# Cross-attention of 16 batches: a scale of v for each group, beta added in two parts, and g made ahead of the third and fourth products

## The reference

```python
q = jnp.einsum('bte,ef->btf', emb, Wq) + bq
k = jnp.einsum('bml,le->bme', latent, Wk) + bk
v = jnp.einsum('bml,le->bme', latent, Wv) + bv
w = jnp.einsum('bte,bme->btm', q, k) * scale
w = jax.nn.softmax(w, axis=1)
pred = jnp.einsum('btm,bme->bte', w, v)
x = pred + emb
mu = jnp.mean(x, axis=-1, keepdims=True)
var = jnp.var(x, axis=-1, keepdims=True)
return (x - mu) * jax.lax.rsqrt(var + EPS) * gamma + beta
```

## Time and profile before

| | |
|---|---|
| median of 3 runs | 228.85 us (227.89 to 231.82) |
| the profiled execution | 228.07 us, its span 226.2 us |
| mean granted clock of TensorE, of full speed | 0.957 |
| busy in the span: PE, DVE, ACT, POOL | 190.5 us (84%), 169.3 (75%), 162.7 (72%), 142.0 (63%) |
| moved from and to HBM | 22.15 MB read, 16.78 MB written |

### The profile page before, as it was taken

How to read it: one execution, slowest core, us unless ns; L and a number is a source line. 1 busy time by engine, 2 the same in 40 slices (tenths; PEclk the granted TensorE clock), 3 DMA queues, 4 the chain that set the end, 5 groups by cost and what they waited for, 6 DMA issues and landing times.

```text
span 226.2 us, 3278 instructions
## 1 busy us (share of the span) xinstructions
PE 190.5 (84%) x1003; PEld 117.6 (52%) x1003; DVE 169.3 (75%) x403; ACT 162.7 (72%) x336; POOL 142.0 (63%) x149
## 2 busy tenths in 40 slices
PE   6994998899996999999999999999999969696100
PEld 6993655465554565656565656555656535342000
DVE  0698138979899896959695969586958686879891
ACT  2745638378968797978797879787978876748730
POOL 1010005103994969696969696969696969698991
PEclk9999599999999999999999999999999999999855
DMA  5999940014018090909090909090909090404175
GB/s 220 315 313 250 398 198 1 3 14 172 0 81 293 0 346 28 352 22 351 23 355 17 352 19 351 23 336 36 348 26 352 19 351 25 185 0 187 67 294 197
DMA packets 9277, 39.14 MB, mean 173 GB/s; under 512 B 812, under 2 KB 2732, under 8 KB 5420
## 3 DMA queue, kind: packets, MB, share of 16 engines
...
HBM read 22.15 MB, written 16.78 MB: 172 GB/s over the span
## 4 chain that ended last, share of the span: by engine, by line
PE 40%; POOL 16%; DVE 14%; ACT 9%; issue 8%; DMA 7%; SPq 2%; POOLq 1%; ACTq 0%; DVEq 0%
PE s_ps L400 16%; DMA ctx_nat<-in_ctx 7%; POOL obuf L925 7%; PE xT_ps L371 6%; POOL obuf L931 5%; PE a_ps L363 5%; PE a_ps L390 4%; PE b_ps L390 4%; DVE obuf L721 4%; PE cg_ps L352 4%; ACT xT L501 3%; ACT obuf L534 2%; POOL rstd L954 2%; ACT prob_part L513 2%; DVE obuf L746 2%
## 5 line engine op out<-in xcount | busy, mean ns | idle before, releaser
L925 POOL TENSOR_TENSOR obuf<-obuf,gamma_all 128x512 f32<-128x512 f32 x43 | 54.2, 1276 | 24.9 <-ACT obuf L534 24.9
L400 PE MATMUL s_ps<-xT,gT 128*120 128x512 f32 x128 | 58.9, 604 | 0.0
L931 POOL TENSOR_TENSOR obuf<-obuf,beta_all 128x1536 f32<-128x1536 f32 (+1 forms) x15 | 49.6, 3306 | 1.2
L501 ACT ACTIVATE xT<-xT_ps 128x512 f32<-128x512 f32 x64 | 34.6, 593 | 17.3 <-PE xT_ps L371 17.3
L534 ACT ACTIVATE obuf<-obuf,shift,rstd 128x512 f32<-128x512 f32 x43 | 33.4, 813 | 9.0 <-POOL shift L958 9.0
L371 PEld LDWEIGHTS xT_ps<-ident,xbuf 128*128 128x128 f32 x256 | 30.1, 142 | 15.1 <-issue 8.0
L371 PE MATMUL xT_ps<-ident,xbuf 128*128 128x128 f32 x256 | 34.0, 275 | 3.8 <-ACT xT L501 3.8
L400 PEld LDWEIGHTS s_ps<-xT,gT 128*120 128x120 f32 x128 | 23.5, 188 | 25.6 <-issue 23.7
L528 ACT ACTIVATE square_junk<-obuf,y_sum 128x512 f32<-128x512 f32 x46 | 32.8, 716 | 0.0
L390 PE MATMUL b_ps<-v_part,prob_part 120*128 120x512 f16 x90 | 24.5, 381 | 4.9 <-DVE obuf L721 4.9
L680 DVE TENSOR_REDUCE s_max<-s_ps 120x1 f32<-120x512 f32 x16 | 11.0, 689 | 20.3 <-PE s_ps L400 20.3
...
## 6 DMA issues: line engine op xcount, KB each, us to landing
...
```

Of the source, the lines that this page charges most:

```text
L400: mm = pe.matmul(s_ps[0:M, :], gT[:, b // 2 % 2, e, b % 2 * M:(b % 2 + 1) * M], xT[:, e, :], start=(e == 0), stop=(e == EC - 1))
L501: act.activation(xT[:, e, :].rearrange("p (j q) -> p j q", q=P), xT_ps[e % 2][:], ACT.Copy)\
L925: pool.tensor_tensor(obuf[:, b % ORING, j, :], obuf[:, b % ORING, j, :], gamma_all[:], ALU.mult)\
L931: pool.tensor_tensor(obuf[:, b % ORING, 0:n, :], obuf[:, b % ORING, 0:n, :], beta_all[:].unsqueeze(1).broadcast_to([P, n, E]), ALU.add)\
```

## The change

**The scales of v.** v gets a scale for each group of contexts: `onto_v`, `back_y` and `bv_scaled` have four columns or rows. So group 0's are made from the bounds of context 0, Wv and bv alone, and those of groups 1 to 3 in a second pass, behind v of batch 0. The loads of wv, bv and x of batch 1 go ahead of contexts 2 and 3. The bound of context 1 moves from ACT to DVE, those of contexts 2 and 3 move on ACT into round 1. ACT makes the high part of wv ahead of round 1's copies of x. POOL reduces three times, and its key products wait for the second pass. DVE's three further rows `bv_scaled` are made at the end of round 2.

**The round.** On PE, g comes ahead of the third and fourth products, v follows them directly (in round 15, v of batch 15 ahead of that of batch 14, for which `nth_v` counts), and the turning of the context moves into the scores, between the second and the third of their four steps. On ACT and DVE the parts of v come ahead of those of the context. On DVE the second residual comes ahead of the centring. On POOL beta is added to two tiles ahead of the statistics and to the third behind them; the store waits for both.

```diff
             load_x(0)
+            sp.dma_start(wv[:], Wv.rearrange("(c p) e -> p c e", p=P)).then_inc(wv_in, 16)
+            sp.dma_start(bv_all[:], bv.partition_broadcast(P)).then_inc(bv_in, 16)
             load_ctx(1)
-            sp.dma_start(wv[:], Wv.rearrange("(c p) e -> p c e", p=P)).then_inc(wv_in, 16)
+            load_x(1)
             load_ctx(2)
             load_ctx(3)
-            sp.dma_start(bv_all[:], bv.partition_broadcast(P)).then_inc(bv_in, 16)
-            load_x(1)
             load_x(2)
             sp.dma_start(gamma_all[:], gamma.partition_broadcast(P)).then_inc(gamma_in, 16)
             sp.dma_start(beta_all[:], beta.partition_broadcast(P)).then_inc(beta_in, 16)
...
-                sp.wait_ge(pool_out, b + 1)
+                sp.wait_ge(pool_out, 2 * (b + 1))
                 sp.wait_ge(dve_out, dve_units_before(b + 1))
                 sp.dma_start(out[b].rearrange("(p j) e -> p j e", j=RJ), obuf[:, b % ORING])\
                     .then_inc(stored[b % ORING], 16)
...
-            def scores(b):
+            def scores(b, next_pair=None):
+
                 if b > 0:
                     pe.wait_ge(prob_low, b)
                 for e in range(EC):
+                    if e == 2 and next_pair is not None:
+                        pe.wait_ge(ctx_in_sem[2 * next_pair // IN_GROUP], 16)
+                        turn_ctx(next_pair)
                     pe.wait_ge(g_copied, EC * (b // 2) + e + 1)
                     pe.wait_ge(xT_copied, EC * b + e + 1)
...
-                if last >= 0:
-                    product(last, 2)
-                    product(last, 3)
                 if s == 1:
                     context_g(1, 0, cg_ps)
                     context_g(1, 1, b_ps)
                 elif s < B - 2:
                     context_g(s // 2 + 1, s % 2, cg_ps)
-                context_v(s - 1)
+                if last >= 0:
+                    product(last, 2)
+                    product(last, 3)
                 if s == B - 1:
                     context_v(s)
-                if s % 2 == 1 and (s + 3) // 2 < PAIRS:
-                    pe.wait_ge(ctx_in_sem[(s + 3) // IN_GROUP], 16)
-                    turn_ctx((s + 3) // 2)
-                scores(s)
+                context_v(s - 1)
+                scores(s, (s + 3) // 2 if s % 2 == 1 and (s + 3) // 2 < PAIRS else None)
```

ACT and DVE, in the start and in the rounds:

```diff
-            bound_ctx(1)
             qk_to_high(3)
             ctx_to_high(1)
             copy_xT(0, 0)
-            bound_ctx(2)
             copy_xT(0, 1)
             act.wait_ge(back_g_done, 1)
-            act.wait_ge(dots_done, LC + 1 + EC)
+            act.wait_ge(dots_done, 1 + LC + 1)
             copy_g(0, 0, a_ps)
             copy_xT(0, 2)
             copy_xT(0, 3)
+            act.wait_ge(dots_done, LC + EC)
             copy_g(0, 1, b_ps)
-            bound_ctx(3)
+            act.wait_ge(wv_in, 16)
+            act.wait_ge(scales_done, 2)
+            act.activation(wv_part[:, HIGH], wv[:], ACT.Copy, scale=scale[:, S_WV:S_WV + 1]).then_inc(wv_high, 1)
...
                 if s == 1:
-                    act.wait_ge(scales_done, 2)
-                    act.activation(wv_part[:, HIGH], wv[:], ACT.Copy, scale=scale[:, S_WV:S_WV + 1]).then_inc(wv_high, 1)
+                    bound_ctx(2)
                 probs_to_high(s - 1)
                 copy_xT(s, 2)
                 copy_xT(s, 3)
+                if s == 1:
+                    bound_ctx(3)
                 if norm >= 0:
                     normalise(norm, 1)
                     normalise(norm, 2)
@@ -593,11 +603,13 @@
                     copy_g(s // 2 + 1, s % 2, cg_ps)
                 if y >= 0:
                     square(y, 0)
+                if s == B - 1:
+                    v_to_high(s)
+                v_to_high(s - 1)
+                if s == 1:
+                    act.wait_ge(scales_done, 3)
                 if s % 2 == 1 and (s + 3) // 2 < PAIRS:
                     ctx_to_high((s + 3) // 2)
-                v_to_high(s - 1)
-                if s == B - 1:
-                    v_to_high(s)
...
             key_dot(0)
-            softmax_bias(0)
+            dve.wait_ge(ctx_in_sem[1], 16)
+            dve.tensor_reduce(own_bound[0:M, B_CTX1:B_CTX1 + 1], ctx_nat[:, IN_GROUP:2 * IN_GROUP, 0:L], AX.XY, ALU.add,
+                              apply_absolute_value=True).then_inc(own_ctx, 1)
             dve.wait_ge(max_bounds, 2)
             dve.wait_ge(bv_bounded, 1)
...
+            dve.tensor_copy(bound[:, S_WV:S_WV + 1], max_bound[:, B_WV:B_WV + 1])
+            scales(dve.scalar_tensor_tensor(bound[:, S_V0:S_V0 + 1], max_bound[:, B_CTX0:B_CTX0 + 1],
                                             max_bound[:, B_WV:B_WV + 1], bv_bound[:], ALU.mult, ALU.add))
-            exact_scales(S_CTX1, S_V + 1)
+            exact_scales(S_WV, S_V0 + 1)
             dve.wait_ge(scales_done, 2)
-            softmax_scale(0)
+            scales(dve.tensor_tensor(back_v[:, 0:1], back[:, S_CTX0:S_CTX0 + 1], back[:, S_WV:S_WV + 1], ALU.mult))
+            dve.tensor_scalar(onto_v[:, 0:1], back_v[:, 0:1], scale[:, S_V0:S_V0 + 1], None, ALU.mult)\
+                .then_inc(back_v_done, 1)
+            dve.tensor_scalar(back_y[:, 0:1], back[:, S_V0:S_V0 + 1], 1.0 / PROB_SCALE, None, ALU.mult)\
+                .then_inc(back_v_done, 1)
+            dve.tensor_scalar(bv_scaled[:, 0], bv_all[:], scale[:, S_V0:S_V0 + 1], None, ALU.mult)\
+                .then_inc(back_v_done, 1)
+            softmax_bias(0)
             dve.wait_ge(wv_high, 1)
...
+            dve.wait_ge(max_bounds, 3)
+            dve.tensor_copy(bound[:, S_CTX1:S_CTX1 + 3], max_bound[:, B_CTX1:B_CTX1 + 3])
+            scales(dve.tensor_scalar(bound[:, S_V1:S_V1 + 3], max_bound[:, B_CTX1:B_CTX1 + 3],
+                                     max_bound[:, B_WV:B_WV + 1], bv_bound[:], ALU.mult, ALU.add))
+            exact_scales(S_CTX1, S_V1 + 3)
+            dve.wait_ge(scales_done, 3)
+            dve.tensor_scalar(back_g[:, 1:GROUPS], back[:, S_CTX1:S_CTX1 + 3], back[:, S_QK:S_QK + 1], None,
...
                 softmax_bias(s - 1)
                 residual(y, 0)
                 softmax_scale(s - 1)
+                residual(y, 1)
                 if norm >= 0:
                     center(norm, RJ - 1, norm + 1)
-                residual(y, 1)
                 probs_to_low(s - 1)
                 residual(y, 2)
                 residual(y, 3)
                 if norm >= 0:
...
+                if s == IN_GROUP + 1:
+                    dve.wait_ge(back_v_done, 2 + 3 + GROUPS - 1)
+                if s == B - 1:
+                    copy_v(s)
                 copy_v(s - 1)
                 statistics(y)
+                if s == B - 1:
+                    v_to_low(s)
+                v_to_low(s - 1)
                 if s % 2 == 1 and (s + 3) // 2 < PAIRS:
                     ctx_to_low((s + 3) // 2)
-                v_to_low(s - 1)
-                if s == B - 1:
-                    copy_v(s)
-                    v_to_low(s)
...
+                if s == 2:
+                    for g in range(1, GROUPS):
+                        dve.tensor_scalar(bv_scaled[:, g], bv_all[:], scale[:, S_V1 + g - 1:S_V1 + g], None, ALU.mult)\
+                            .then_inc(back_v_done, 1)
```

POOL:

```diff
-            pool.wait_ge(own_late, 1)
+            pool.wait_ge(own_wv, 1)
+            pool.partition_all_reduce(max_bound[:, B_WV:B_CTX1], own_bound[:, B_WV:B_CTX1], P,
+                                      bass.bass_isa.ReduceOp.max).then_inc(max_bounds, 1)
             pool.wait_ge(own_ctx, GROUPS - 1)
             pool.partition_all_reduce(max_bound[:, B_CTX1:], own_bound[:, B_CTX1:], P,
...
+            pool.wait_ge(back_v_done, 5)
             key_multiply(1)
             key_multiply(2)
...
-            def plus_beta(b):
-                n = pool_units(b)
-                pool.wait_ge(pool_gamma, units_before(b + 1))
-                pool.tensor_tensor(obuf[:, b % ORING, 0:n, :], obuf[:, b % ORING, 0:n, :],
-                                   beta_all[:].unsqueeze(1).broadcast_to([P, n, E]), ALU.add)\
+            def plus_beta(b, first, end):
+                pool.wait_ge(pool_gamma, units_before(b) + end)
+                pool.tensor_tensor(obuf[:, b % ORING, first:end, :], obuf[:, b % ORING, first:end, :],
+                                   beta_all[:].unsqueeze(1).broadcast_to([P, end - first, E]), ALU.add)\
                     .then_inc(pool_out if b < B - 2 else last_out[b - B + 2][0], 1)
 
             def finish_statistics(b):
@@ -963,11 +998,13 @@
                     key_multiply(s)
                 if s >= 3:
                     times_gamma(s - 3)
-                    plus_beta(s - 3)
+                    plus_beta(s - 3, 0, 2)
                 finish_statistics(s - 2)
+                if s >= 3:
+                    plus_beta(s - 3, 2, 3)
             finish_statistics(B - 1)
             times_gamma(B - 2)
-            plus_beta(B - 2)
+            plus_beta(B - 2, 0, 1)
```

(1 more changed line is left out.)

77 lines of the change are left out of this document (39 added, 38 removed).

## The result

| | before | after |
|---|---|---|
| median of 4 runs, us | 228.84 (227.89 to 231.82) | 216.63 (216.36 to 216.84) |
| profiled execution: span, us | 226.2 | 214.8 |
| round 1 starts at | 31.13 | 24.83 |
| round 5 starts at | 77.85 | 69.70 |
| round 13 starts at | 167.86 | 159.79 |

The ratio is 0.948 [0.945, 0.951] (the brackets are a 95% interval): faster, and faster than the range that was given. The direction and the wait were foretold, the sizes not: 222.5 was forecast. Executions more than 1.5% above the fastest of their kernel count in the medians of this document, not in its ratios.

A forecast was written before the change was run, and what follows sets the result against it. PE's round and POOL's loop, about equally long, were taken to bound the kernel. After the change, with x's ring setting pairs, 182.9 + 5 L gave 219.9, 6.3 under the 226.2 span; 228.85 - 6.3 = 222.5 us, range 218 to 227.5.

The forecast's parts named there:

- the wait: Odd rounds from 7: PE idle about 1 us at the first transposes, released by the DMA of x.
- the first rival: Middle rounds: x is not late, PE sets the pair at 21.98; 217.9 on the runs' scale; chance 0.2.
- The start: Before round 1: PE's 3.55 us stand goes and the clock is 2.4 GHz, saving 1.2 and 1.35; sum 6.1.
- The fourth product's wait: PE's round: the fourth product's 0.49 wait for DVE's second residual goes; a v wait of 0.46 comes.
- POOL's loop: POOL's round: splitting beta cuts it from 11.1 to about 10.2 us, so it no longer binds.
- the ring of x: Middle rounds: squares, statistics, beta's third tile, store, then load of x; 15.62 + L sets the pair, at 23.0.
- PE's loss to x: Odd rounds: x ready at 23.0 while PE is at 21.98, so PE waits about 1.0 us.
- L: Landing time of a load of x on SP's queue: 7.4 us, the median of 16 loads.
- the sum: Whole span: 71.85 + 4 x (15.62 + L) + (14.15 + L) + 34.4 = 182.9 + 5 L; 219.9 at L = 7.4.
- Net 0.1 given back: Up to round 5: new DVE work and an ACT wait, 1.5 + 1.2 + 0.6, against 3.2 saved; bounds 0 and 3.
- the 34.4: From round 15's start to the span's end: 36.17 less 2.52 plus 0.75.
- 0.23 a round: PE's new order: a pair of 21.98 against 22.44, a gain if PE sets it.

The follow-up runs named there:

- lf_both_old: Changed kernel with x's load ahead of the store, g back behind the third and fourth products and centring back ahead of the second residual: 216.84 us, ratio 0.949.
- load_first: Changed kernel with each load of x put ahead of the store before it on SP's queue: 214.60 us, ratio 0.937 to the kernel before.
- beta_one_load_first: Changed kernel with beta added in one part ahead of the statistics and x's load ahead of the store: 221.15 us, ratio 0.964.
- start_only: Changed kernel with every move inside the rounds and beta's split taken back, leaving the scale of v per group: 221.86 us, ratio 0.967.
- beta_one: Changed kernel with beta added in one part again, ahead of POOL's statistics: 220.83 us, ratio 0.964 to the kernel before.
- beta_one_dot_early: Changed kernel with beta in one part and the key dot of batch 3 moved from the end of round 3 to round 2's: 220.24 us, ratio 0.959.
- lf_turn_first: Changed kernel with x's load ahead of the store and the context's turning back ahead of the scores, round 1 apart: 214.93 us, ratio 0.940.
- lf_g_late: Changed kernel with x's load ahead of the store and g back behind the third and fourth products: 212.75 us, ratio 0.930.
- lf_centre_first: Changed kernel with x's load ahead of the store and the centring back ahead of the second residual: 214.76 us, ratio 0.939.

## Why the prediction was wrong

It was 5.9 us too high: 5.1 in the span, and 0.8 because it put the median above the profiled execution, as before; the profiled execution of after took 216.64, its median. Of the 5.1, 2.15 are before round 5, 2.4 in rounds 5 to 14 and 0.5 at the end. The result is also below the 217 to 219 of the first rival, in which x is not late: it lies in the 0.06 that was left for a kernel faster than all.

**Right: the mechanism.** The start lost its wait and its half clock (6.3 us, forecast as 6.1). The fourth product's wait became v's (0.32 by its row in lf_both_old, 0.30 in load_first, each with some 0.17 of overlap to add; forecast as 0.49 and 0.46). POOL's loop went off the path with the split, and the ring of x came in its place: load_first against beta_one_load_first shows both. The ring's own length, 15.62 forecast, is 15.54. PE's loss to x is 0.55 a pair (22.53 against 21.98), where 1.0 was forecast.

**Mis-sized: L, the time from a load's issue until PE has x.** The prediction chose 7.4, the median of before; it is 7.0 in every pair, which is 5 x 0.4 = 2.0 us (the ring's own 0.08 a pair is 0.4 more). With 7.0 the sum gives 217.9 of span. The fit that the prediction quoted from the Trainium skill (DMA: Bandwidth & Descriptors, Anatomy of one DMA — SWDGE (gpsimd) path) made it an estimated 6.4, so the measurement lies between. The trace of before could have said so. The 7.4 is a median over all 16 loads, and the first ones, at the start, have 10.2 to 17.3; over the eleven that stand right behind a store it is 7.1, and four of these have 6.9, as the load of 169.30:

```profile
DMA to landing us min/median/max: 6.9/6.9/6.9
```

The load of 158.0, the one with 8.6 in the earlier trace rows, and the traffic behind it, by windows with the DMA engines' share and rate as their last two columns:

```profile
158.00 0.43 SPq L262 DMA_DIRECT2D xbuf<-in_x  x1
...
164.00:164.50 0.50, 0.50 (x4) 0.38 (x3) 0.00 (x0) 0.50 (x2) 0.50 (x2) 1.00 0.63 262
164.50:164.80 0.30, 0.30 (x2) 0.11 (x1) 0.17 (x1) 0.30 (x1) 0.30 (x1) 1.00 0.20 55
164.80:165.10 0.30, 0.30 (x2) 0.18 (x1) 0.30 (x1) 0.26 (x2) 0.30 (x1) 1.00 0.00 0
...
165.50:166.60 1.10, 1.10 (x4) 0.39 (x3) 1.06 (x3) 1.10 (x3) 1.10 (x1) 1.00 0.00 0
```

All bytes had moved by 164.8, 6.8 after the issue (2.1 MB since 157.5 by such windows, the store and the load); the landing shown is 1.8 later. Landings of 8 us and more right behind a store are shown only in kernels whose pair is not set by x (before, start_only, beta_one, beta_one_dot_early). Why the shown landing runs behind the traffic there stays open.

**The step that failed: that up to round 5 only the start counts.** "Net 0.1 given back" is right, as a total, for the start alone (start_only, 46.84 for 46.82). But the moves and the split work in rounds 1 to 4 as well, and I priced them from round 5 on. Against start_only they gave 2.0, of which 1.25 stand in rounds 3 and 4 (24.43 to 23.18). There the split alone is worth 0.8, because a shorter beta no longer meets the key dot of batch 3 (beta_one_dot_early), and the two moves alone 0.95 (lf_both_old); the two overlap, since together they are 1.25. The other 0.7 lie in rounds 1 and 2, within the scatter of kernels with the same lists, and no run separates them.

**The end** came out 0.5 below the 34.4: the statistics began at 10.34, where the squares' 10.4 and 0.09 were forecast, and the rest of the way was 0.4 dearer than before instead of 0.75.

**Wrong without a price.** The new order was to give PE 0.23 a round if PE set it. Where PE does set the pair, the order gives nothing: 22.00 with both moves taken back (lf_both_old), 21.98 with the turning back ahead of the scores (lf_turn_first), 21.98 as changed. Two figures were read loosely: x was due at 120.2 for round 9, which began at 122.68, so it had 2.5 us to spare, not 3; and slower by 2% needs L above 9.6, not 10.

Not foreseen as a choice: of the two moves against the fourth product's wait, the second residual ahead of the centring does it alone (a pair of 21.13 in lf_g_late, against 22.00 with neither). g ahead of the products only trades that wait for v's, alone (21.97, lf_centre_first) or with the other (21.98, load_first), since it gives up its place as cover for the third residual. That is 0.42 a round, which lf_g_late has back.
